# One-hots of the gather passes: halves in pass one, node numbers from a PSUM bank in passes two and three, and an earlier first norm

## The reference

```python
# layer 0, four times: sum of neighbours, two matrices
agg = segment_sum(x[src], dst);  x = relu((x + agg) @ W1 + b1) @ W2 + b2
# layer 1: messages by relation, mean over the neighbours of each relation
out = x @ root + bias;  out += segment_sum((x @ W[r])[src] of edges of type r, dst) / count
# layer 2: 16 relations made of 8 bases; each edge weighted by a sigmoid
srcs = alphas[rels] * (x @ w_rel)[rels, src];  relu(sum over dst + in-degree * (x @ update))
# layer 3: 8 relations, gated
msg = (x @ W)[rel, src] + bias[rel];  relu(segment_sum(msg * gate, dst) + x @ loop)
```

## Time and profile before

| | |
|---|---|
| median of 3 runs | 2515.14 us |
| lowest, highest | 2513.55, 2516.49 us |
| span of the profiled execution | 2514.1 us |
| PE, weight load, DVE, ACT, POOL busy | 58%, 37%, 37%, 25%, 55% of the span |

### The profile page before, as it was taken

One profiled execution on the slowest core, in us unless ns is written; L12 is line 12 of the kernel. 1 busy time (PEld: TensorE's weight loads), 2 busy tenths in 40 slices (PEclk: granted clock), 3 DMA queues, 4 the chain that ended last, 5 costly groups with the idle time before them and its releaser, 6 DMA issues.

```text
span 2514.1 us, 29639 instructions
## 1 busy us (share of the span) xinstructions
PE 1448.2 (58%) x6376; PEld 942.7 (37%) x6481; DVE 919.5 (37%) x2242; ACT 632.7 (25%) x1671; POOL 1387.3 (55%) x1541
## 2 busy tenths in 40 slices
PE   5666599999988065555555154555544333333333
PEld 3333355455444044434433043334333233333333
DVE  6999622122116932223222443333332222122221
ACT  0677400000013043333333154334444000000000
POOL 1000015230211877777776677777776577777776
PEclk8888799999999577677767577665667666655565
DMA  0000001000026133233333222222222222122221
GB/s 19 0 0 0 17 14 11 7 5 0 6 51 252 37 105 104 87 104 103 104 105 97 71 77 76 67 76 76 75 74 62 65 54 53 52 54 54 54 54 46
DMA packets 120618, 148.86 MB, mean 59 GB/s; under 512 B 74779, under 2 KB 88737, under 8 KB 117362
## 3 DMA queue, kind: packets, MB, share of 16 engines
q0 software_dynamic: 40000, 81.89, 12.5%
q1 hardware_dynamic: 80562, 66.31, 8.0%
HBM read 91.39 MB, written 56.72 MB: 59 GB/s over the span
## 4 chain that ended last, share of the span: by engine, by line
POOL 46%; PE 26%; issue 17%; DVE 6%; ACT 3%; DMA 1%; POOLq 1%; SPq 0%; DVEq 0%; ACTq 0%
POOL adj L803 46%; PE acc L1047 16%; PE acc L938 4%; PE acc L1130 2%; ACT adj L1300 1%; ACT acc L1304 1%; DVE feat L1598 1%; PE acc L1194 1%; DMA adj<-table,adj 1%; PE misc L982 1%; PE acc L1160 1%; DVE adj L1926 0%; DMA table<-adj 0%; ACT adj L1379 0%; DVE adj L1897 0%
## 5 line engine op out<-in xcount | busy, mean ns | idle before, releaser
L803 POOL DMA_INDIRECT adj<-table,adj x1248 | 1256.7, 1007 | 441.1 <-issue 377.9
L1194 PE MATMUL acc<-adj 128*128 x2640 | 540.9, 382 | 728.1 <-ACT adj L1379 345.6
L1194 PEld LDWEIGHTS acc<-adj 128*128 128x128 f32 x2640 | 487.9, 282 | 796.9 <-issue 796.5
L1585 DVE TENSOR_TENSOR adj<-node_iob,drel 128x768 f32<-128x768 bf16 (+1 forms) x222 | 210.2, 949 | 624.5 <-PE acc L1194 624.3
L1379 ACT ACTIVATE adj<-adj 128x128 f32<-128x128 f32 x832 | 263.0, 389 | 601.1 <-DMA adj<-table,adj 517.1
L1047 PE MATMUL acc<-adj,feat 128*128 (+2 forms) x2042 | 401.3, 354 | 6.6 <-DVEq L1634 3.5
L753 POOL TENSOR_TENSOR node_rep<-node_rep,compb 128x128 f32<-128x128 f32 x128 | 57.1, 446 | 555.0 <-DMA node_rep<-in_L_gnn_weight_dram 546.2
L1047 PEld LDWEIGHTS acc<-adj,feat 128*128 (+1 forms) x2100 | 185.8, 98 | 213.3 <-issue 4.7
L1160 PE MATMUL acc<-adj 128*128 128x512 f32 (+1 forms) x350 | 193.4, 697 | 74.9 <-ACT adj L1394 74.9
L938 PE MATMUL acc<-feat 128*128 128x400 bf16 x625 | 147.1, 396 | 78.8 <-ACT acc L1304 61.9
L1598 DVE TENSOR_SCALAR feat<-feat 128x400 bf16<-128x400 int16 x625 | 156.1, 316 | 0.0
(11 more groups left out here) (264 smaller groups left out, 1015.7 us busy)
## 6 DMA issues: line engine op xcount, KB each, us to landing
table<-adj SPq DMA_DIRECT2D x50, 512.0 KB, 2.8
table<-adj SPq DMA_DIRECT2D x25, 1024.0 KB, 4.2
adj<-table,adj POOLq DMA_INDIRECT x1250, 2.5
table<-adj SPq DMA_DIRECT2D x25, 64.0 KB, 1.6
temp<-in_x_dram SPq DMA_DIRECT2D x6, 256.0 KB, 3.2
out_dram<-adj SPq DMA_DIRECT2D x24, 64.0 KB
wrel<-node_rep SPq DMA_DIRECT2D x16, 64.0 KB, 3.0
adj<-in_L_gnn_W_dram SPq DMA_DIRECT2D x2, 512.0 KB, 5.0
```

The costliest lines, as they stand in the source:

```text
L803: pool.indirect_dma_start(ring[:, p_, 0:D], None, table, bass.IndirectOffsetOnAxis(ap=gidx[:, p_:p_ + 1], axis=0)).then_inc(msgs_in[u.r][c ...
L1194: last = nc.tensor.matmul(acc[:, bass.ds(blk[s], width)], hot[:, c, j, :], ring_flat[:, bass.ds(place[s], width)], start=False, stop=True, ...
L1585: return nc.vector.tensor_tensor(o, node_iob[:, :].unsqueeze(1).to_broadcast([P, n, P]), drel[:, bass.ds(s, n)].unsqueeze(2).to_broadcast( ...
```

## The change

It does four things. In pass 1 `hot_group` issues two one-hots of three steps each in place of one of six. In passes 2 and 3 the one-hot reads the node numbers from PSUM: bank 6, free since pass 1, gets an f32 copy of them between the passes. The first norm of `first_nodes` waits for x alone, and the wait for the tables and the bias (`tab_in`, 48) moves behind it on DVE and becomes PE's own before its first transpose. Counts that PE and ACT load from memory for their waits are masked with 1023.

```diff
--- before.py
+++ after.py
@@ -57,6 +57,7 @@
 CHUNKS = (TURNS - 1) * len(SIZES) + 2
 FIRST = AHEAD_T * len(SIZES)
 BANK3 = 3
+NODES_BANK = 6
 
 SL = 8
 SLICES = D // SL
@@ -77,6 +78,7 @@
 FSLOTS = 3
 TURN = 4 * FSLOTS
 COUNT_MAX = 255
+COUNT_MASK = 1023
 PARTS3 = 3
 KB = 512
 CH = -(-NA // KB)
@@ -85,6 +87,7 @@
 SLOTS = 3
 USES = [len(range(s, QB, SLOTS)) for s in range(SLOTS)]
 BANKS = 5
+assert max(FSTEPS, TILES, PAIRS) <= COUNT_MASK
 assert TQ * TC == TILES and NI * QB == BLOCKS and TURNS == BLOCKS and (BLOCKS - 1) * P < NA <= NP
 assert (TURNS - 1) * SPT + LASTG * LASTNB == STEPS and (TURNS - 1) * TPT + SIZES[0] + SIZES[1] == TILES
 assert 2 * KB + D + 1 <= BANK3 * KB and TURNS % AHEAD_T == 1
@@ -336,6 +339,7 @@
 
         acc = ps("acc", [P, 7 * KB])
         misc = ps("misc", [P, KB])
+        node_ps = acc[:, NODES_BANK * KB:NODES_BANK * KB + P]
         fslots = [acc[:, i * 2 * KB:(i + 1) * 2 * KB].rearrange("p (k c) -> p k c", k=2)[:, :, 0:FCOLS]
                   for i in range(FSLOTS)]
         pads_set = sem("pads_set")
@@ -370,6 +374,7 @@
         indeg_clear = sem("indeg_clear")
         ends_ready = sem("ends_ready")
         hot_ready = sem("hot_ready")
+        nodes_set = sem("nodes_set")
 
         foh_ready = sem("foh_ready")
         fstep_done = sem("fstep_done")
@@ -933,7 +938,7 @@
                 places, turns_ = vals[0:AHEAD], vals[AHEAD:]
                 for q in range(FNB):
                     pe.wait_ge(foh_ready, k * FNB + (q + 1))
-                    pe.wait_ge(zeroed, turns_[q])
+                    pe.wait_ge(zeroed, turns_[q] & COUNT_MASK)
                     for j in range(FG):
                         nc.tensor.matmul(acc[:, bass.ds(places[q * FG + j], FCOLS)], flo[:, q, :, j], foh[:, q, j, :],
                                          start=False, stop=True, skip_group_check=True).then_inc(fstep_done, 1)
@@ -1129,7 +1134,7 @@
                             pe.wait_ge(bank_free[b], bank_use(i, q, j) + 1)
                             nc.tensor.matmul(acc[:, b * KB:b * KB + c1 - c0], xTb[:, q, :], tab[:, c0:c1],
                                              start=True, stop=True).then_inc(bank_full[b], 1)
-                pe.wait_ge(tab_set, 1)
+                pe.wait_ge(tab_in, 48)
                 nodes(pe, body)
 
                 pe.wait_ge(xTb_ready, BLOCKS + 2)
@@ -1177,7 +1182,7 @@
                     pe.wait_ge(msgs_in[u.r][k], msgs_before(ph, u, k) + 16 * SIZES[k])
                 for c, n in enumerate(sizes):
                     if ph < 3:
-                        pe.wait_ge(tiles_in, upto[c] + (ph - 1) * TILES)
+                        pe.wait_ge(tiles_in, (upto[c] & COUNT_MASK) + (ph - 1) * TILES)
                     elif c == 0:
                         if isinstance(t.k, int) and t.num() == 0:
                             landed(t, 0)
@@ -1267,7 +1272,7 @@
                     pe.wait_ge(prod_free[j], BLOCKS)
                 pe.wait_ge(sum_read, BLOCKS)
                 pair_weights()
-                pe.wait_ge(tab_set, 2)
+                pe.wait_ge(tab_set, 1)
                 one_pass(2, general)
                 for j in (0, 1, 4):
                     pe.wait_ge(prod_free[j], 2 * BLOCKS)
@@ -1296,7 +1301,7 @@
             hold(act, ends_set, 2)
 
             def copy_out(i, r, end):
-                hold(act, fstep_done, end + AHEAD)
+                hold(act, fstep_done, (end & COUNT_MASK) + AHEAD)
                 nc.scalar.activation(adj[:, :, bass.ds(i * (TURN * 2 * FB) + r * 2 * FB, 2 * FB)].rearrange("p h (k n) -> p h k n", k=2),
                                      fslots[r % FSLOTS].rearrange("p k (h n) -> p h k n", n=FB), ACT.Copy).then_inc(flushed, 1)
 
@@ -1580,10 +1585,10 @@
             nc.vector.tensor_reduce(peak_row[0:1, P:P + 1], off_f[:, 0, :], AXX, ALU.max)
             nc.vector.engine_nop().then_inc(ends_ready, 1)
 
-            def one_hot(o, s, n):
+            def one_hot(o, numbers, s, n):
 
                 return nc.vector.tensor_tensor(
-                    o, node_iob[:, :].unsqueeze(1).to_broadcast([P, n, P]),
+                    o, numbers.unsqueeze(1).to_broadcast([P, n, P]),
                     drel[:, bass.ds(s, n)].unsqueeze(2).to_broadcast([P, n, P]), ALU.is_equal)
 
             link(nc.vector.tensor_copy(node_iof[:, :, :], node_io[:, :].unsqueeze(2).to_broadcast([P, P, FG])))
@@ -1651,7 +1656,7 @@
                     sizes = groups_of(t)
                     for c, n in enumerate(sizes):
                         dve.wait_ge(ggroup_free, z * GROUPS + t.num(NB, c + 1))
-                        one_hot(hot[:, c, 0:n, :], t.num(SPT, c * sizes[0]), n).then_inc(ghot_ready, 1)
+                        one_hot(hot[:, c, 0:n, :], node_iob[:, :], t.num(SPT, c * sizes[0]), n).then_inc(ghot_ready, 1)
                 turns(dve, body)
 
             def merge(l):
@@ -1756,6 +1761,7 @@
                         freed(nc.vector.tensor_tensor(rest[:, b1, :].rearrange("p b f -> p (b f)"), bk[2][:, 0:D], rows[:, 0, :], ALU.add), 2)
                 for n_ in range(NORMS):
                     norm(0, n_)
+                dve.wait_ge(tab_in, 48)
                 nodes_ahead(dve, body)
 
             def hot_group(ph, t, c):
@@ -1766,7 +1772,12 @@
                     dve.wait_ge(group_free, before.num(NB, (ph - 1) * GROUPS + c + 1))
                 else:
                     after(dve, group_free, (ph - 1) * GROUPS)
-                one_hot(hot[:, c, 0:sizes[c], :], t.num(SPT, c * sizes[0]), sizes[c]).then_inc(hot_ready, 1)
+                at_, half = t.num(SPT, c * sizes[0]), sizes[c] // 2
+                if ph == 1:
+                    one_hot(hot[:, c, 0:half, :], node_iob[:, :], at_, half)
+                    one_hot(hot[:, c, half:2 * half, :], node_iob[:, :], t.num(SPT, c * sizes[0] + half), half).then_inc(hot_ready, 1)
+                else:
+                    one_hot(hot[:, c, 0:sizes[c], :], node_ps, at_, sizes[c]).then_inc(hot_ready, 1)
 
             def block_sum(ph, t, b, general):
 
@@ -1968,13 +1979,15 @@
                 nc.vector.memset(near_i[:, :], -1)
                 nc.vector.memset(kinds_i[:, :], 0).then_inc(near_pads, 1)
                 dve.wait_ge(x_in, 32)
-                dve.wait_ge(tab_in, 48)
-                nc.vector.engine_nop().then_inc(tab_set, 1)
                 first_nodes()
                 dve.wait_ge(small_in, SMALL * 16)
                 dve.wait_ge(xn_ready, BLOCKS)
                 edge_weights()
                 one_pass(1, general)
+                if not general:
+                    dve.wait_ge(prod_free[2], BLOCKS)
+                    nc.vector.tensor_copy(node_ps, node_io[:, :]).then_inc(nodes_set, 1)
+                    dve.wait_ge(nodes_set, 1)
                 gate_constants()
                 pair_weights()
                 one_pass(2, general)
```

## The result

The changed kernel took **2469.5 us** (median of 4 runs, 2467.42 to 2471.15) beside 2514.35 us for the kernel before in the same comparison (2513.08 to 2516.49): a ratio of 0.9815, 95% interval 0.9804 to 0.9827, 44.9 us less. The forecast was 2473. All lines after L938 have moved by a few: L803 is now L808, L1585 is L1590, L1828 and L1835 are L1839 and L1846.

What follows compares the result with a forecast made beforehand. POOL's indirect gathers were taken to bound the kernel. The terms -34.7 + 1.5 - 8.6 - 2 + 1.5 = -42.3 us, taken from 2515.1, gave 2473 us; range 2464 to 2481, extended to 2485 for the first rival.

Steps and rivals of the forecast that it cites:

- What bounds: Three gather passes: POOL's pace of 1.248 us a gather bounds; DVE one-hots with both inputs in SBUF hold gathers.
- Part 1: Passes 2 and 3: one-hots reading node numbers from PSUM hold no gather; gain 34.7 us, bounds 28 and 38.
- the room taken: Passes 2 and 3: gathers freed from one-hots may meet other DVE operations; +1.5 us, bounds 0 and 4.
- Near 1 us: Pass 3: sign that the stretch of POOL's gather line falls to near 1 us instead of 18.2.
- about 5: Pass 2: sign that the stretch of POOL's gather line falls to about 5 us instead of 20.2.
- Part 2: Pass 1: two one-hots of 384 instead of one of 768; gain 8.6 us, bounds -2 (a loss) and 11.
- Each half holds for itself: Pass 1: a held gather gets through between the halves, costing 0.14 us a group instead of 0.27.
- the formula: Gather passes: average hold is (operation's length less 0.13 us) squared over 2 x 1.25; 0.27 us for a 957 ns one-hot.
- loses to the second half: Pass 1 rival: a held gather waits through the second half too, gaining nothing or losing 2 us; 2482 us, chance 0.12.
- Part 3: First norm waits for x alone: PE starts up to 3.7 us earlier; gain 2 us, bounds 0 and 3.7.
- Part 4: Between the passes: the copy of the node numbers on DVE is covered by a 25.57 us wait and costs nothing.
- Part 5: Adjacency matrix construction: masks on loaded counts are mostly hidden in waits; costs 1.5 us, from 0 to 10.

Runs made afterwards that it cites:

- e2_halves: Kernel before plus the count masks and pass 1 one-hots in halves; ratio 1.0008 to the kernel before, which took 2762.15 us there.
- e11_halves: Kernel before plus the count masks and pass 1 one-hots in halves, on another chip; ratio 0.9997 to the kernel before, 2745.07 us there.
- e5_after_again: The changed kernel once more, unaltered, as an anchor; 2471.8 us beside 2514.55 for the kernel before, ratio 0.9825.
- e8_swap: The changed kernel with the operands of each one-hot in the other order; 2468.2 us, ratio 0.9818 to the kernel before.
- e1_masks: Kernel before plus the masks on loaded counts and nothing else; ratio 0.9984 to the kernel before, which took 2762.15 us there.
- e9_masks: Kernel before plus the masks alone, on another chip; ratio 0.9998 to the kernel before, which took 2745.07 us there.

## Why the prediction was right, and where its terms were off

- **What bounds, and why a pass is longer than its pace: right.** POOL's line carries 45% of the chain, and pass 3, in which only short operations of DVE still have two inputs in SBUF, has 0.8 us of stretch.
- **Part 1, -34.7 with +1.5 for the room taken, so -33.2: measured -32.0** (-14.6 and -17.4; pass 2 without the 1.7 us of L1846 gives -16.3, and the prediction had -16.5 for it). The one-hot's time was right (955 ns), and so was the room: L1846, a holder as before, took 5.6 us where it had taken 3.9, and the prediction allowed it up to 6.4. "Near 1 us" for pass 3 came out as 0.8, and "about 5" for the long window of pass 2 as 354.15 - 368 x 0.944 = 6.8. The prediction counted 12 gathers that start inside L1828 with 0.14 us or more of it left; the trace has 20, none of them stretched, so the reading stands on more than it said.
- **Part 2, -8.6: measured -7.8; the step held in this execution, but it is no rule.** "Each half holds for itself" is what nearly every gather of the changed kernel's pass 1 shows. Two of its gathers (DVE, POOL; x2 is the pair of halves):

```profile
1154.66 1.30 POOL L808 DMA_INDIRECT adj<-table,adj  x1 [0.30 <-issue]
...
1154.59 1.03 DVE L1590 TENSOR_TENSOR adj<-node_iob,drel 128x384 f32<-128x384 bf16 x2 [3.55 <-PE acc L1199]
```

```profile
1278.75 1.41 POOL L808 DMA_INDIRECT adj<-table,adj  x1 [0.30 <-issue]
...
1278.33 1.02 DVE L1590 TENSOR_TENSOR adj<-node_iob,drel 128x384 f32<-128x384 bf16 x2
```

  The gather of 1154.66 starts 0.07 us into the pair and gets through at the seam: the first half ends at 1154.59 + 0.55 = 1155.14, and the gather ends 0.82 us later, at 1155.96. The one of 1278.75 starts 0.42 us in and so asks (0.13 us later) when the first half has just ended; it ends 0.81 us after the second half, 1279.35 + 0.81 = 1280.16. In this pass all that start 0.07 to 0.41 us into a pair pass at the seam; from 0.42 to 0.47 two pass and three wait. `e2_halves` has the case that breaks the step:

```profile
1067.36 0.34 DVE L1812 TENSOR_SCALAR adj<-adj 128x128 f32 x1
...
1067.61 1.02 DVE L1586 TENSOR_TENSOR adj<-node_iob,drel 128x384 f32<-128x384 bf16 x2
1067.95 1.51 POOL L804 DMA_INDIRECT adj<-table,adj  x1 [0.30 <-issue]
```

  This gather starts 0.34 us in and asks at 0.47, before the first half ends at 0.55, and yet it waits for the second. So do all twelve of `e2_halves` and all nine of `e11_halves` that start 0.33 to 0.35 us into a pair, while ten in the changed kernel, `e5_after_again` and `e8_swap` that start at 0.32 to 0.41 pass at the seam. In each of the 21 the pair follows directly on L1812, but two of the ten follow the same operation (L1817 there) as closely, so what decides is open.

  By the formula a pair costs 0.16 us a group if every gather that asks before the seam passes there (the prediction's 0.14 took both halves to hold for up to 0.55 - 0.13 = 0.42 us, and the second one does for up to 1.03 - 0.55 = 0.48), and 0.20 us if those from 0.33 us on wait; a whole one-hot costs 0.27.

  Measured, the pairs held the gathers of pass 1 for 10.0 us in the changed kernel, 10.3 in `e5_after_again`, 12.2 in `e8_swap`, 13.0 in `e11_halves` and 15.4 in `e2_halves`, where whole one-hots had 15.6 to 18.8. So -7.8 is luck in part. The rival "loses to the second half" is true for a part of the gathers, and the expectation of `e11_halves`, which takes 0.32 us for a border, doesn't fit the ten.
- **Part 3, -2: measured -1.1.** x was in 9.7 us after its issue (739.25 - 729.52), where the prediction had 7.8 (746 from 738.17). So the norm came 2.35 us earlier and PE's first transpose 2.3 us, instead of 3.7 (each counted from the issue of x). And ACT now waits 2.80 us for its first slot, against 0.70: half of it was given back there, as foreseen. That the 1.1 us are all of this part is not shown: by the profiles compared above it is worth about half a us.
- **Part 4, 0:** the wait between passes 1 and 2 grew by 0.8 us, in which I can't tell the copy from PE's end of the pass.
- **Part 5, +1.5: not borne out, and the largest error of the sum.** In the profiles the construction's last slot is cleared at 295.0 us before and at 286.3 to 291.2 us in all thirteen kernels with masks (287.7 in the changed kernel, 288.9 and 289.4 in the two with the masks alone). So the masks cost nothing there, and x's load comes 3.7 to 8.7 us earlier, 8.65 in the changed kernel. The granted clock alone does not explain it: its mean from 70 to 290 us is 0.86 before, 0.88 in the changed kernel, and 0.86 in `e1_masks` too. By the medians it is less: -44.9 in all, less the -39.8 + 1.1 - 1.1 of the rest, leaves -5 us; by their ratios `e1_masks` had -4.4 us and `e9_masks` -0.5, the latter not to be told from none. That the masks are the cause is not shown: a kernel with the other parts and without them wasn't tried, and there is only one profile of before, which may lie high by chance.
- **The sum.** The parts in the passes and the norm gave 39.8 us where -33.2 - 8.6 - 2 = -43.8 was written, 4 us less; the construction gave some 5 us where +1.5 was written. The two errors are of opposite sign, and 2469.5 for 2473 owes its closeness in part to that.

## What to carry to other kernels

If GpSimd issues indirect DMAs and bounds a stage, look on DVE's timeline for two-input operations with both inputs in SBUF, and put one input into PSUM where a bank is free: here it cost DVE nothing (955 for 957 ns) and freed the whole hold. Cutting the operation in two is the second-best: it saved 7 to 47% of the hold, by how the gathers fell. Of two long operations cut into eight pieces, one let its gathers through and the other did not. Price the bank, and read what the price is made of: 8 of 10 us came back here at the end of the pass, 2.8 of them as waits for the shared bank's copy (two of the three perhaps not needed) and some 3 at a lower granted clock.

## What the runs showed of the hardware that I had not expected

- At the seam of two DVE operations that follow each other directly a waiting gather isn't always let in. Of those that started 0.32 to 0.41 us into a pair of halves ten were let in and 21 were not, and one gather waited 6.09 us through eight pieces of an addition. What decides is open.
- The same kernel on the same input has executions of 2514 and of 2745 to 2762 us. PE's waits for nothing in its line of the gather passes are 58.0 us in the kernel before at 2514 and 357.5 in `e1_masks`, and the gathers' packets end as early in both, in the median 2.2 us after the start. A comparison in which the kernel before takes another time than it did is worth its counts (how long a gather is held), not its ratio.
